# First-half tails of the third attention in banks of their own, row maxima ahead of norms, queries and values copied by ScalarE, routing places moved forward

## The reference

```python
x = x + L0_conv(gn(x))             # neighbourhood attention, 8 heads
x = x + L1_conv(gn(x))             # routed region attention, 5x5 convolution, two layer norms
t = tokens(x)
t = t + L2_attn(ln(t))             # "third attention": windows of 128, 4 heads, causal band of 32
t = t + L2_ffn(ln(t))              # 8 experts, top 2, GELU
t = t + L3_attn(ln(t))
t = t + L3_ffn(ln(t))              # 8 experts with a capacity

def L2_attn(x):                    # per window of 128 tokens
    q, k, v = split(x @ Wqkv)      # 4 heads of 32
    a = softmax(q @ k.T * SCALE + band_mask)
    return (a @ v) @ Wproj + bproj
```

## Time and profile before

| | |
|---|---|
| median of 3 runs | 527.66 us (524.83 to 527.77) |
| profiled execution | 527.12 us, span 525.4 us |
| mean granted TensorE clock | 0.910 |
| busy: PE / DVE / ACT / POOL | 460.5 / 320.3 / 226.0 / 167.7 us |

### The profile page before, as it was taken

The page is one execution under the profiler, slowest core; times in us unless marked ns, Lnnn a source line. Parts: engine busy times, 40 slices in busy tenths (PEclk is TensorE's granted clock), DMA queues, the critical chain, the costliest instruction groups (busy, mean ns, idle before and its releaser), DMA issues.

```text
span 525.4 us, 10346 instructions
## 1 busy us (share of the span) xinstructions
PE 460.5 (88%) x3619; PEld 346.4 (66%) x3619; DVE 320.3 (61%) x891; ACT 226.0 (43%) x522; POOL 167.7 (32%) x229
## 2 busy tenths in 40 slices
PE   4988999796999999998797887999970999889984
PEld 3276777433577777776677777999960644477973
DVE  3968878477956676947637634672434550557466
ACT  0848787264155655553413204755520234210630
POOL 7722217103412332325213037257716400021000
PEclk9999999899699999999767758999995899969997
DMA  7000000000000000008000033868613100000001
GB/s 289 15 2 2 1 2 1 1 2 1 1 1 1 2 1 1 2 2 320 1 1 1 20 95 87 191 164 197 197 44 121 75 0 0 1 1 0 1 1 40
DMA packets 13692, 24.80 MB, mean 47 GB/s; under 512 B 1954, under 2 KB 7914, under 8 KB 13130
## 3 DMA queue, kind: packets, MB, share of 16 engines
q1 hardware_dynamic: 12170, 21.12, 12.1%
q0 software_dynamic: 1472, 3.02, 3.2%
HBM read 21.12 MB, written 3.01 MB: 46 GB/s over the span
## 4 chain that ended last, share of the span: by engine, by line
PE 74%; DVE 12%; ACT 5%; issue 4%; DMA 1%; POOL 1%; DVEq 1%; POOLq 0%; ACTq 0%
PE ps L1106 67%; PE ps L1249 3%; PE ps L1116 2%; DVE tabs L1830 1%; ACT arena L1030 1%; POOL arena L787 1%; PE ps L1229 1%; DVE st L1813 1%; DMA xT<-in_xT_dram 1%; DVE arena L1958 1%; DVE tabs L1998 1%; PE ps L1565 1%; DVE oK L1934 1%; DVE nmx L2060 1%; DVE st L1794 1%
## 5 line engine op out<-in xcount | busy, mean ns | idle before, releaser
L2060 DVE TENSOR_REDUCE nmx<-ps 128x1 f32<-128x512 f32 x64 | 43.7, 686 | 22.3 <-PE ps L1106 21.9
L949 ACT ACTIVATE pT<-ps 128x512 f32<-128x512 f32 x64 | 38.2, 597 | 40.1 <-PE ps L1106 39.5
L1106 PE MATMUL ps<-kr,qr 128*128 128x320 f32 (+3 forms) x136 | 46.2, 403 | 4.4 <-DVE kr L1985 2.4
L778 POOL DMA_INDIRECT arena<-expert_rows_dram,row_of x30 | 31.1, 1037 | 47.4 <-DVE row_of L2213 37.5
L1030 ACT ACTIVATE arena<-ps,tabs 128x128 f32<-128x128 f32 x120 | 34.1, 369 | 27.4 <-PE ps L1106 25.6
L1958 DVE CUSTOM_DVE_ANT_0 arena<-ps,tabs 128x320 f32<-128x320 f32 (+1 forms) x64 | 28.8, 458 | 14.7 <-PE ps L1106 14.7
L579 POOL TENSOR_TENSOR rstd<-ve,nhalf 128x4 f32<-128x4 f32 (+2 forms) x17 | 15.5, 912 | 62.4 <-DVE ve L1823 62.0
L1106 PE MATMUL ps<-pT,tabs 128*32 128x128 f32 (+2 forms) x576 | 34.7, 293 | 0.7 <-ACT pT L949 0.7
L675 POOL TENSOR_TENSOR tabs<-vaug,ones 128x151 f32<-128x151 f32 x32 | 14.2, 445 | 64.5 <-PE ps L1106 36.7
L1106 PEld LDWEIGHTS ps<-kr,qr 128*128 128x128 f32 x136 | 25.5, 198 | 12.9 <-issue 5.7
L1106 PE MATMUL ps<-fw,arena 128*128 x240 | 32.0, 276 | 1.3 <-ACT arena L1030 1.3
(11 more groups left out here) (356 smaller groups left out, 1124.9 us busy)
## 6 DMA issues: line engine op xcount, KB each, us to landing
fw<-in_m_w_dram SPq DMA_DIRECT2D x3, 2048.0 KB, 8.0
xT<-in_m_w_dram SPq DMA_DIRECT2D x16, 256.0 KB
cT<-in_m_w_dram SPq DMA_DIRECT2D x14, 256.0 KB
expert_out_dram<-arena SPq DMA_DIRECT2D x30, 64.0 KB, 3.3
convw<-in_convw_dram SPq DMA_DIRECT2D x1, 1600.0 KB, 11.1
rows<-in_rows_dram SPq DMA_DIRECT2D x1, 584.0 KB, 7.0
xT<-in_xT_dram SPq DMA_DIRECT2D x1, 512.0 KB, 3.6
expert_rows_dram<-tabs SPq DMA_DIRECT2D x2, 256.0 KB, 4.6
```

What stands on the lines that cost most here:

```text
L778: pool.indirect_dma_start(out=x_rows[:, i, :], out_offset=None, in_=x_dram[h], in_offset=bass.IndirectOffsetOnAxis(ap=row_of[:, h, i:i + 1 ...
L949: act.activation(pT[:, u % 8, :], ps[:, 4 + u % 2, :], ACT.Exp).then_inc(S("n1_p"), 1)
L1106: return pe.matmul(dst, lhsT, rhs, start=start, stop=stop, skip_group_check=True)
L2060: dve.tensor_reduce(nmx[:, s // NH8, s % NH8:s % NH8 + 1], ps[:, s % N1_S, :], AX.X, ALU.max, negate=True).then_inc(S("n1_nmx"), 1)
```

## The change

- The tails of tiles 0 to 3 get banks 6 and 7 (`n2_tail`): transposed output in columns 0 to 127, projection in columns 128 to 255. Tiles 4 to 7 keep banks 4 and 5. The products with the values of tiles 2 and 3 now wait for the normalisation of tile t - 2; the wait for the residual addition moves to the transposes of tiles 2 and 3, and the transpose of tile 0 waits for the last addition of the second attention.
- VectorE's list: maxima 1, 2 and 3 come ahead of a gain, of the statistics of tile 7 and of its last addition; normalisations 1, 2, 3 come ahead of norms and residual additions.
- ScalarE copies both halves' values and the second half's queries. The second half's queries use bank 2 (before 6), its keys bank 3 (before 7).
- TensorE's list: in the first half, products with values come ahead of the tails' transposes and projections; the second half's turn comes ahead of projection 2, its queries and keys ahead of projection 3. `m2_turn(0)` and the first router come ahead of the transposes of tile 4, scores 5 behind `m2_turn(0)`, `routed_places(0)` behind scores 7. Warm-up products before scores 5: 20 before, 6 after. From there to `routed_tokens(0)`: 14 before, 10 after.

```diff
--- before
+++ after
@@ -472,6 +472,9 @@
...
         y_dram = [nc.dram_tensor(f"expert_out_{h}_dram", (TH * P, P), F32, kind="Internal").ap() for h in range(2)]
+
+        def n2_tail(t):
+            return ps[:, 6 + t % 2, 0:2 * P] if t < 4 else ps[:, 4 + t % 2, 2 * P:4 * P]
@@ -935,7 +938,14 @@
...
                 act.wait_ge(*at("n2_k_ps", i + 1))
-                act.activation(halves(bT)[i], ps[:, (4, 7)[i], :], ACT.Copy).then_inc(S("n2_k"), 1)
+                act.activation(halves(bT)[i], ps[:, (4, 3)[i], :], ACT.Copy).then_inc(S("n2_k"), 1)
+
+            def n2_values(i):
+                act.wait_ge(*at("n2_v_ps", i + 1))
+                if i == 0:
+                    act.wait_ge(*at("ones_cols", 3))
+                act.activation(vaug4[:, 4 * i:4 * i + 4, :, 0:HD4], ps[:, (5, 0)[i], :].rearrange("p (t h d) -> p t h d", t=4, h=NH4),
+                               ACT.Copy).then_inc(S("n2_v"), 1)
@@ -954,6 +964,8 @@
...
                     n2_keys(0)
+                if s == N2_PRODUCTS + 3:
+                    n2_values(0)
@@ -982,7 +994,7 @@
...
                 act.wait_ge(*at("n2_ot", t + 1))
-                act.activation(oT[:, P * t:P * t + P], ps[:, 4 + t % 2, 2 * P:3 * P], ACT.Copy).then_inc(S("n2_oT"), 1)
+                act.activation(oT[:, P * t:P * t + P], n2_tail(t)[:, 0:P], ACT.Copy).then_inc(S("n2_oT"), 1)
@@ -995,9 +1007,12 @@
...
             n2_output(2)
+            n2_turned(1, 1)
             n2_output(3)
-            n2_turned(1, 1)
+            act.wait_ge(*at("n2_q_ps", 2))
+            act.activation(halves(aT)[1], ps[:, 2, :], ACT.Copy, scale=HD4 ** -0.5).then_inc(S("n2_q"), 1)
             n2_keys(1)
+            n2_values(1)
             n2_exp(4)
@@ -1386,9 +1401,9 @@
...
                 if i:
-                    pe.wait_ge(*at("n1_add", T))
-                mm(ps[:, (2, 6)[i], :], w2a[:, 0:P], halves(nT)[i]).then_inc(S("n2_q_ps"), 1)
-                mm(ps[:, (4, 7)[i], :], w2a[:, P:2 * P], halves(nT)[i]).then_inc(S("n2_k_ps"), 1)
+                    pe.wait_ge(*at("n2_pta", 4))
+                mm(ps[:, 2, :], w2a[:, 0:P], halves(nT)[i]).then_inc(S("n2_q_ps"), 1)
+                mm(ps[:, (4, 3)[i], :], w2a[:, P:2 * P], halves(nT)[i]).then_inc(S("n2_k_ps"), 1)
@@ -1422,7 +1437,9 @@
...
                 pe.wait_ge(*at("n2_v", t // 4 + 1))
-                if t >= 2:
+                if t in (2, 3):
+                    pe.wait_ge(*at("n2_o", t - 1))
+                if t >= 4:
                     pe.wait_ge(*at("n2_add", t - 1))
@@ -1431,12 +1448,16 @@
...
                 pe.wait_ge(*at("n2_o", t + 1))
-                pe.transpose(ps[:, 4 + t % 2, 2 * P:3 * P], oK[:, t % 2, :], ident[:, :]).then_inc(S("n2_ot"), 1)
+                if t == 0:
+                    pe.wait_ge(*at("n1_add", T))
+                if t in (2, 3):
+                    pe.wait_ge(*at("n2_add", t - 1))
+                pe.transpose(n2_tail(t)[:, 0:P], oK[:, t % 2, :], ident[:, :]).then_inc(S("n2_ot"), 1)
...
                 pe.wait_ge(*at("n2_oT", t + 1))
-                mm(ps[:, 4 + t % 2, 3 * P:4 * P], oT[:, P * t:P * t + P], w2p[:, :]).then_inc(S("n2_proj"), 1)
+                mm(n2_tail(t)[:, P:2 * P], oT[:, P * t:P * t + P], w2p[:, :]).then_inc(S("n2_proj"), 1)
@@ -1502,7 +1523,7 @@
...
             pe.wait_ge(*at("n1_add", T - 1))
-            keep_busy(6, 6)
+            keep_busy(3, 6)
             n2_turn_p(0)
@@ -1511,42 +1532,42 @@
...
             n2_back(0)
+            n2_with_values(2)
             n2_turn_p(3)
             n2_project(0)
-            n2_with_values(2)
             n2_back(1)
+            n2_with_values(3)
             n2_project(1)
-            n2_with_values(3)
             n2_back(2)
+            n2_turn(1, 1)
             n2_project(2)
-            keep_busy(4, 6)
             n2_back(3)
+            n2_queries_keys(1)
             n2_project(3)
-            n2_turn(1, 1)
-            keep_busy(4, 3)
-            n2_queries_keys(1)
             n2_values(1)
-            keep_busy(6, 3)
+            keep_busy(3, 1)
             n2_scores(4)
+            m2_turn(0)
             n2_scores(5)
-            m2_turn(0)
+            router("m2", 0, 7, oT, "nb_T", range(0, 4))
+            keep_busy(1, 6)
             n2_turn_p(4)
-            router("m2", 0, 7, oT, "nb_T", range(0, 4))
             n2_scores(6)
+            keep_busy(1, 6)
             n2_turn_p(5)
...
             n2_scores(7)
+            routed_places(0)
             n2_turn_p(6)
             n2_with_values(5)
-            keep_busy(6, 6)
-            routed_places(0)
             n2_back(4)
+            keep_busy(2, 6)
             n2_turn_p(7)
...
             n2_with_values(6)
-            keep_busy(8, 6)
+            keep_busy(6, 6)
             routed_tokens(0)
@@ -2031,10 +2052,6 @@
...
             evac_values("l1_v_ps", "l1_v", (1, 2), vaug_heads, w_fold[:, 3, :])
-            def n2_queries(i):
-                dve.wait_ge(*at("n2_q_ps", i + 1))
-                dve.tensor_scalar(halves(aT)[i], ps[:, (2, 6)[i], :], HD4 ** -0.5, None, ALU.mult).then_inc(S("n2_q"), 1)
-
             for s in range(HEADS + N1_V + 9):
@@ -2061,7 +2078,8 @@
...
                 if s == N2_PRODUCTS + 2:
-                    n2_queries(0)
+                    dve.wait_ge(*at("n2_q_ps", 1))
+                    dve.tensor_scalar(halves(aT)[0], ps[:, 2, :], HD4 ** -0.5, None, ALU.mult).then_inc(S("n2_q"), 1)
                 if s == N2_PRODUCTS + 3:
@@ -2074,9 +2092,6 @@
...
                     residual("n1t_ps", "n1_tok", (6, 7), bK, "L1_conv_bo_a", (s - 3,))
-            def n2_values(i):
-                evac_values("n2_v_ps", "n2_v", (5, 0), lambda i: vaug4[:, 4 * i:4 * i + 4, :, 0:HD4], halves_of=(i,))
-
             def n2_maxima(t):
@@ -2091,52 +2106,48 @@
...
                 dve.wait_ge(*at("xb2_ready", t // 4 + 1))
-                dve.tensor_tensor(aK[:, t, :], ps[:, 4 + t % 2, 3 * P:4 * P], aK[:, t, :], ALU.add).then_inc(S("n2_add"), 1)
+                dve.tensor_tensor(aK[:, t, :], n2_tail(t)[:, P:2 * P], aK[:, t, :], ALU.add).then_inc(S("n2_add"), 1)
...
             n2_maxima(0)
-            gain_tile("ln1", bK, "L1_conv_ln1_g", 7)
             for t in range(4, 7):
...
             n2_maxima(1)
-            dve.wait_ge(*at("ones_cols", 3))
-            n2_values(0)
+            gain_tile("ln1", bK, "L1_conv_ln1_g", 7)
             for t in range(4, 7):
...
             add_tile("ln1", bK, cK, 7)
+            n2_maxima(2)
             stats_after("ln2", cK, "ln1", 7, 8)
             mean_of("ln2", 7)
-            n2_maxima(2)
+            n2_normalise(0)
             stats_after("na", aK, "ln2", 4, 7)
...
             gain_tile("ln2", cK, "L1_conv_ln2_g", 7)
-            n2_normalise(0)
+            n2_maxima(3)
             add_tile("ln2", cK, aK, 7)
...
             mean_of("na", 7)
-            n2_maxima(3)
+            n2_normalise(1)
             for t in range(4, 7):
                 normalise_tile("na", aK, bK, t)
-            n2_normalise(1)
             n2_residual(0)
+            n2_normalise(2)
             normalise_tile("na", aK, bK, 7)
-            n2_normalise(2)
             n2_residual(1)
+            n2_normalise(3)
             nb_stats(0)
-            n2_normalise(3)
+            nb_stats(1)
             n2_residual(2)
-            nb_stats(1)
             nb_stats(2)
...
                 mean_of("nb", t)
-            n2_queries(1)
-            n2_values(1)
             n2_maxima(4)
...
             n2_maxima(5)
```

## The result

The changed kernel takes 0.987 of the time before (95% interval 0.985 to 0.990), from 20 executions of each: about 6.6 us less than 527.1, so 520.5 where 518.0 was forecast. Executions of both kernels fall into two groups some 8 us apart (4 of 20 in the upper one before and 11 of 20 after; 22 of 58 and 3 of 7 among the later executions), the ratio compares the lower groups, the medians over all, 527.77 and 526.87, therefore hardly differ, and the profiled execution of the changed kernel (529.33 us, span 527.6, clock 0.90) belongs to the upper one. It is read by stages, each counted from the start of scores 0 (the first product of `bandr` and `identr` behind the second attention), and its end is taken apart at the close of this document.

What follows compares the result with a forecast made beforehand. It took the kernel to be bound by a serial chain at half clock, VectorE's work between maxima, and GpSimd; 8.3 (queries' copy) + 0.0 (second half's order) + 0.9 (warm-ups) = 9.2 us off 527.1 gave 518.0, range 511.5 to 523.5.

Steps and rivals of the forecast that it cites:

- (b): Second half gives back: scores 5 behind the norms and two warm-ups delay the tables 3.2 us; 521; chance 0.21 with (c).
- (c): First half's tails don't come apart; only the maxima's 2.0 and eight warm-ups' 3.6 us remain; 521.5; chance 0.21 with (b).
- The maxima: First half, VectorE: earlier row maxima and values copied by ScalarE start exponentials 3 2.0 us earlier.
- The tails: First half, TensorE: separate banks cut a tile's round from 3.78 to about 2.2 us; queries' copy ends at 264.8, 8.3 earlier.
- rival (a): Clock stays high through the first half, the end of the four normalisations comes 10.8 us earlier; 513.3; chance 0.18.
- the eight warm-ups: First half, TensorE: warm-up products taken off the path to the second half's queries, 3.6 us.
- The queries' copy at 0: Second half's queries copied by ScalarE instead of VectorE: same cost, 0.60 us, so no gain from the move.
- T0 is the queries' copy plus 7.3: Second half: T0, the end of VectorE's four normalisations, follows the queries' copy by 7.3 us, so comes 8.3 earlier.
- The second half's order at 0: Second half, TensorE: scores 5 moved back and routing places moved forward together bring 0, ends -2 and +3 us.
- The 0.9 for two warm-ups fewer: Ahead of the routed tokens, six warm-ups instead of eight save 0.9 us at low clock, 0.5 at full.
- "I let the rest move along": Behind the row-number cast: nothing hangs on absolute time, so the whole 9.2 us gain reaches the end.
- Rival (d): Slower: without warm-ups the clock stays low through the second half and into the expert stage; 529; chance 0.06.

Runs made afterwards that it cites:

- the copies' run: Changed kernel with the first half's values copy and second half's queries and values copies back on VectorE; no ratio, expert stage 90.6 us.
- table early: Changed kernel plus one Gelu on a spare 128x1 tile behind the first router's exponentials, loading ScalarE's table early; ratio 0.985 to the kernel before.
- both with the old order: Changed kernel plus early Gelu, with TensorE's old second-half order and its eight warm-ups instead of twelve ahead of the turned half; ratio 0.986 to the kernel before.
- the first run: The changed kernel profiled and timed once more, unchanged; ratio 0.990 to the kernel before.

## Why the prediction was right, and where it was off

It said 518.0, between 511.5 and 523.5, and faster by over 1%. It is 520.5, faster by 1.3%. The forecast gave 9.2 us at the cast and everything behind it for free; measured are 8.0 at the cast and 6.6 at the end. Rivals (b) and (c) named 521 and 521.5, nearer than 518.0, but by ways that the runs don't show: that the figure lies beside theirs is chance.

- **The maxima: right.** 2.0 us at exponentials 3 by the forecast, 2.02 measured (12.46 to 10.44). Of these the order is 1.42; the values' copy carries 0.6 only beside the old order and 0.1 beside the new.
- **The tails: right in mechanism and sum, wrong in its parts.** Queries' copy at 264.8 was the forecast, 21.2 us after scores 0; the profiles have 20.0 and 21.2. The clock was let fall at 257.2, 13.6 us after scores 0: the profile in which it does so is the one with 21.2. The other, with the clock high for 1.7 us more, goes a part of the way to rival (a). But I gave 2.7 us to the banks with their order and 3.6 to the eight warm-ups; undone one at a time they cost 4.6 to 5.8 and 1.6 to 2.8. Each compared with the profile of the changed kernel whose clock first fell most nearly alike, banks, warm-ups, maxima's order and copies cost 4.6, 1.6, 2.7 and 2.3 us at the queries, 11.1 together, where the whole is 8.4. The parts don't add, and that two mis-sized ones gave the right sum is luck.
- **The queries' copy at 0: wrong term, hidden by a good sum.** It is ScalarE that makes the copy in the changed kernel, so the sum came to no harm, but its place is worth something: VectorE's own wait for projection 3 would have cost some 2.2 us. I saw the projection go behind the queries and followed only the means for GpSimd's root, not what VectorE's list would hold up had the copy stayed there.
- **T0 is the queries' copy plus 7.3: right** (7.33 in both profiles, 7.2 to 7.9 in the other runs), with the four normalisations at 3.10 us beside GpSimd's work.
- **The second half's order at 0: right within 1 us, by the pairs with and without it.** Slots 0.6 us earlier after T0 (forecast 1.3), turn 7 at T0 + 15.7 (forecast 15.3), residual addition 4 at T0 + 17.3 where it was at 16.6. **The 0.9 for two warm-ups fewer** didn't arrive: T0 to cast is 26.2 and 26.4, 26.4 and 25.6 before. What the sum left out is the clock behind T0, low for 10.3 us where it was low for 7; the 12 warm-ups at the turn, which keep it high, show what that costs. Rival (b) is refuted in its size, 3.2 us, though its sign is there: the one-hot tables start at T0 + 19.1 and 19.4, but 18.5 and 17.7 before.
- **"I let the rest move along": the step that failed**, and one of the prediction's own signs of being wrong, in milder form (the cast 8 us earlier, the end 6.6). Of 8.0 us at the expert stage's start 5.3 are left at its end. In the changed kernel PE's clock is high for the second group of first-layer products (1.06 us in both profiles, 1.92 in both before), so PE is through with them early, stands still 1.94 us for ScalarE's table load and Gelus, and runs the next 7 us at the low clock; before, PE stood still 0.74 us, and the clock, which had fallen earlier, was low for 3.5. The first group doesn't decide it: in the second profile it ran at the low clock, and the stage lost as much:

```profile
309.92 1.96 PE L1121 MATMUL ps<-arena,xT 128*128 128x128 f32 x8
...
311.82 1.06 PE L1121 MATMUL ps<-arena,xT 128*128 128x128 f32 x8
314.82 1.93 PE L1121 MATMUL ps<-fw,arena 128*128 x8 [1.94 <-ACT arena L1045]
```

A faster PE ahead met the same table load. With the load off the path the stage is 90.4 us, 3.0 to 4.2 less than in the changed kernel's profiles and 0.8 less than before: there is no loss without the load. The load alone doesn't make it: in the copies' run it is there, PE stands still a quarter of a microsecond less, and the loss is not. Why the clock falls in the one and not in the other stays open.
- **Rival (d) holds for one stage.** Its place was wrong: the clock didn't stay low from the first half on, it fell anew where PE waited, at the turned half and in the expert stage. The Trainium skill's rule that it was built on ("TensorE: Matmul & The Clock Gate", Part 1: low is the default, activity releases it) agrees with the trace at the turned half: the clock fell where PE stood still 3.80 us and stayed high where 12 warm-ups filled that, worth 3.6 us at the cast. It doesn't account for the stretch in the last section, where PE was busy.

## What to carry to other kernels

When an edit shortens a chain by microseconds, follow the freed engine to its next fixed cost (here a 1.28 us table load) and ask whether it will now stand still there; two profiles a quarter of a microsecond apart in idling were 2.8 us apart behind it. Warm-up products belong in idle time that something else bounds, as at the turned half; on the path eight of them cost 1.6 to 2.8 us. Take two profiles of each kernel and compare those whose clock falls at the same place: one pair alone put the gain at the cast at 9.7 us, like pairs at 8. Undo the parts one at a time: a sum that comes out can hold two terms that are off by 2 us each.

## What the runs showed that I had not expected

The clock can be at its lower level without PE having stood still. From 415.5 to 436.0 us the changed kernel, and the one with the second half's order back, run the same work of the fourth attention, whose first turned half starts at 401.9 and 402.0 us. The stage tables, first of the changed kernel:

```profile
405.50:415.50 10.00, 10.00 (x41) 5.71 (x39) 4.55 (x6) 3.17 (x5) 3.55 (x4) 1.00 0.01 3
415.50:436.00 20.50, 20.50 (x38) 9.17 (x37) 7.43 (x8) 3.66 (x5) 0.00 (x0) 0.50 0.00 0
```

and of the one with the order back:

```profile
405.00:415.00 10.00, 10.00 (x41) 5.98 (x39) 4.35 (x7) 3.17 (x5) 3.76 (x4) 0.99 0.01 5
415.50:436.00 20.50, 20.50 (x68) 9.79 (x67) 8.52 (x9) 7.08 (x11) 0.00 (x0) 1.00 0.00 0
```

PE is busy throughout in both; one gets 38 matmuls done, the other 68. The stretch lasted 20.5 to 24 us, began some 10 us after the clock had risen, and stands in 5 of the 12 profiles of changed kernels (changed twice, table early, copies back, both with the old order) and in neither of the kernel before; with it the kernel takes 125.5 to 128.5 us from the fourth attention's first turned half to the end, without it 117.9 to 119.1: 7 us and more. The profiles of "table early" and of "both, old order" have it and still count in those kernels' ratios, which are to that extent too high. Since two kernels with the same timing differ in it, it isn't set by the order of work alone. Rival B of the first run, that the change itself puts this stage at the low clock every time, falls with the seven profiles without it, all of kernels that keep most or all of the change; both profiles of the changed kernel as it stands have it, so whether the change makes it more frequent stays open, as does its cause.
